# Turning the identity into unread banks at seven places on TensorE, in a graph layer with edge messages, linear attention and slice attention

## What is computed

```python
xn = layernorm(x)
# edges: a filter from the attributes, times the gathered row, summed by source node
filt = silu(attr @ Wf1 + bf1) @ Wf2 + bf2
agg  = segment_sum(xn[dst] * filt, src)
h    = silu(agg @ Wu1 + bu1) @ Wu2 + bu2
x1   = x + xn + batchnorm(h) + linear_attention(xn) * gate(xn) @ Wproj + bproj
# slices: 8 heads, each with 64 slice tokens, over all nodes
x2   = layernorm(x1)
w    = softmax((x2 @ W_x + b_x) @ W_slice / temp)      # nodes x (8 x 64)
tok  = w.T @ (x2 @ W_fx) / sum(w)                      # slice tokens
attn = softmax((tok @ W_q) @ (tok @ W_k).T / 8)
out  = x1 + (w @ (attn @ (tok @ W_v))) @ W_out + b_out
```

## Time and profile before

| | us |
|---|---|
| median of three runs | 2088.68 |
| lowest and highest of them | 2083.26, 2089.93 |
| the profiled execution's own time | 2100.86 |
| its span, from first to last instruction | 2099.1 |
| TensorE busy | 1882.4 (90%) |
| GpSimd busy | 1443.0 (69%) |
| mean granted TensorE clock | 0.956 |

### The profile page before, as it was taken

The page is one execution under the profiler, slowest core; times in us unless marked ns, Lnnn a source line. Parts: engine busy times, 40 slices in busy tenths (PEclk is TensorE's granted clock), DMA queues, the critical chain, the costliest instruction groups (busy, mean ns, idle before and its releaser), DMA issues. The chain is left out here.

```text
span 2099.1 us, 38406 instructions
## 1 busy us (share of the span) xinstructions
PE 1882.4 (90%) x9844; PEld 1548.4 (74%) x9844; DVE 1501.5 (72%) x3453; ACT 1332.9 (63%) x2412; POOL 1443.0 (69%) x997
## 2 busy tenths in 40 slices
PE   5989999999989998998899889999997298799998
PEld 3667888787778787777777777877786276577778
DVE  6967877777777767776777677776775287788846
ACT  4547776776677667666766576667664067577733
POOL 2216888888888888888888888888888564355600
PEclk9999999999999999999999999999999599699979
DMA  9888888988988798878988898888897793000002
GB/s 370 319 299 169 162 159 166 173 159 143 172 165 160 137 172 168 157 140 162 176 146 154 156 177 142 157 159 167 150 158 115 202 322 120 12 0 0 0 31 103
DMA packets 288979, 325.41 MB, mean 155 GB/s; under 512 B 30118, under 2 KB 251721, under 8 KB 288688
## 3 DMA queue, kind: packets, MB, share of 16 engines
q0 software_dynamic: 112896, 102.81, 40.0%
q1 hardware_dynamic: 172576, 217.21, 32.4%
q10 hardware_dynamic: 3280, 2.83, 0.5%
HBM read 167.64 MB, written 154.97 MB: 154 GB/s over the span
## 5 line engine op out<-in xcount | busy, mean ns | idle before, releaser
L994 POOL DMA_INDIRECT sums<-x_rows,out_idx x784 | 1226.3, 1564 | 288.3 <-issue 207.2
L1048 PE MATMUL bank<-wf,x_rows 128*128 128x256 f32 x3136 | 800.5, 384 | 0.0
L1048 PEld LDWEIGHTS bank<-wf,x_rows 128*128 128x128 f32 x3136 | 545.2, 192 | 54.3
L1172 ACT ACTIVATE x_rows<-bank,bf 128x512 f32<-128x512 f32 x392 | 270.4, 690 | 279.8 <-PE bank L1026 277.1
L1268 DVE TENSOR_TENSOR msg_low<-bank,msg_high 128x512 fp32r<-128x512 f32 x392 | 271.3, 692 | 162.0 <-ACT msg_high L1192 162.0
L1299 DVE TENSOR_TENSOR bank<-bank,x_rows 128x512 f32<-128x512 f32 x392 | 272.7, 696 | 119.4 <-PE bank L1048 114.5
L1046 PE MATMUL bank<-gnn_bf_halves,ones 128*128 128x256 f32 x784 | 296.5, 378 | 0.0
L1192 ACT ACTIVATE msg_high<-bank 128x512 fp32r<-128x512 f32 x392 | 234.3, 598 | 88.5 <-DVE bank L1299 85.8
L1180 ACT ACTIVATE x_rows<-pair 128x516 f32<-128x516 f32 x392 | 234.1, 597 | 63.7 <-DMA sums<-x_rows,out_idx 62.9
L1199 ACT ACTIVATE x_rows<-bank 128x512 f32<-128x512 f32 x392 | 235.2, 600 | 36.9 <-PE bank L1036 33.4
L1036 PE MATMUL bank<-window,spread 128*128 128x256 f32 x784 | 193.2, 328 | 58.2 <-DVE spread L1263 37.2
(11 more groups left out here) (331 smaller groups left out, 2740.2 us busy)
## 6 DMA issues: line engine op xcount, KB each, us to landing
window<-xn_halves SPq DMA_DIRECT2D x392, 128.0 KB, 4.2
sums<-gate SPq DMA_DIRECT2D x32, 800.0 KB, 10.8
x_rows<-id_rows SPq DMA_DIRECT2D x98, 256.0 KB, 5.0
x_rows<-attr_rows SPq DMA_DIRECT2D x98, 256.0 KB, 4.7
xn_halves<-xn_halves SPq DMA_DIRECT2D x7, 1792.0 KB, 7.3
x_rows<-id_rows SPq DMA_DIRECT2D x98, 128.0 KB
sums<-x_rows,out_idx POOLq DMA_INDIRECT x784
res<-sums SPq DMA_DIRECT2D x24, 512.0 KB, 7.7
```

The costliest lines, as they stand in the source:

```text
L994: nc.gpsimd.indirect_dma_start(g.sums_dram[k], bass.IndirectOffsetOnAxis(ap=out_idx[:, ET * c + t:ET * c + t + 1], axis=0), summed[c % 2][ ...
L1048: mm = T.matmul(out, hidT[:, j // 2, f, ds((2 * (j % 2) + t) * P, P)], g.wf2[:, f, :], start=False, stop=f == CB - 1)
L1172: A.activation(hidT[:, h, f, :], hps[:], ACT.Silu, bias=g.bf1[:, f:f + 1]).then_inc(hid_ready, 1)
```

## The change

A new helper turns the identity into a bank that nobody reads at that time, so many times in a row. It is called at seven places on TensorE; nothing else is altered. No instruction waits for these turns, and they give no semaphore. The line numbers behind each place shift by up to 13.

```diff
+def keep_warm(nc, g, bank, n):
+    for _ in range(n):
+        nc.tensor.transpose(bank[:, 0:P], g.ident[:], g.ident[:])
@@ opening, tensor
             gram_group(NG - 1)
+            keep_warm(nc, g, turn[0], 12)
@@ messages_and_attention, tensor
+            keep_warm(nc, g, fps[1], 6)
             hidden(0, 0, 0, 0)
@@ update_nodes, tensor, behind the turns of line 1612
                     mm.then_inc(back_made, 1)
+            keep_warm(nc, g, turn[0], 32)
@@ slice_tokens, tensor
             for t in range(NT - LAG, NT):
+                keep_warm(nc, g, tps, 8 if t == NT - LAG else 3)
                 turn_w(t, t % RING)
                 tokens(t, t % RING)
@@ slice_attention_and_output, tensor
                 mm = T.matmul(g.ps[0][0:FD, ds(q * P, P)], mean_of[:], diag[:, ds(q * P, P)], start=True, stop=True)
             mm.then_inc(mat, 1)
+            keep_warm(nc, g, g.ps[5], 8)
             pe.wait_ge(vec, FX_DONE)
...
                 mm = T.transpose(g.ps[5][0:FG, ds(k * P, P)], at[:, ds(k * FG, FG)], g.ident[:])
             mm.then_inc(mat, 1)
+            keep_warm(nc, g, g.ps[4], 6)
             pe.wait_ge(vec, BACK)
...
                 if h % 4 == 3:
                     mm.then_inc(mat, 1)
+            keep_warm(nc, g, g.ps[4], 6)
             for u in range(NT):
```

## The result

The changed kernel takes 2082.82 us (median of 22 runs, 2079.16 to 2095.09). The kernel before, run in turn with it on the same chip, takes 2091.68 us (22 runs, 2081.98 to 2099.41). The ratio is 0.9966, 95% interval 0.9951 to 0.998, so 4.2 to 10.2 us less, 7.1 by the ratio. The forecast was -9.5 us. The two fastest runs differ by 2.8 us, the medians by 8.9: what goes is above all the slow part of the spread.

A forecast was written before the change was run, and what follows sets the result against it. GpSimd bounds the edge loop; TensorE's stream, slowed by low clock, bounds the attention's last third. Attention -8.5, opening -1, update and tail 0 sum to -9.5 us, carried to the median 2088.68: 2079.2 us, stated range 2073 to 2089.

The forecast's parts named there:

- the attention term: Slice attention: eight turns in the `fxT` wait keep the clock from falling at 2006, so later products run faster; -8.5 us.
- the cover: Ahead of the output products: six turns (0.65) and four products (0.47) fit inside the 1.49 us wait, costing nothing.
- Opening, -1: Twelve turns behind the opening, six ahead of the edge loop: first scatter sooner, -1 us, bounds -3.5 and +2.6.
- Later and shorter: Edge loop's start: the clock still falls behind the six turns, but later and for less than the 10.1 us before.
- 32 turns, 0: Behind the update: clock is low again when the tokens begin, so 0 us; bounds -5.6 and +1.
- the tokens' tail, 0: Eight and three turns in the tokens' tail: clock is 1.00 there anyway, so 0 us, at most +0.3.
- The clock holds and falls soon after: Rival, attention: 64-row products too weak to hold the clock after 2006; about 2086.5 us, chance 0.2.
- My price of nothing: Attention's two groups of six turns lie in covered waits and cost nothing; at the low clock 0.5 and 0.6 us.
- Less to win in most runs: Rival, attention: the median run may have no low stretch, leaving only the opening's -1; about 2087.7 us, chance 0.12.
- Turns do not count: Rival, all seven places: the 81 turns do not raise or hold the clock; about +0.7, 2089.4 us, chance 0.06.
- The 32 turns hold up the block's end: Rival, update's end: turns at the low clock delay it, +1.0 us; with nothing won elsewhere 2089.7 us, chance 0.12.

The follow-up runs named there:

- third group: Beside the kernel before (2087.31 us): four products in the `fxT` wait, 2087.99 us; products at all seven places, 2082.55; changed kernel with four products for the eight turns, 2084.81.
- Eight turns alone: Kernel before plus only the eight identity turns in the slice attention's wait for `fxT`: 2087.30 us, ratio 0.9975.
- four products alone: Kernel before plus only four full identity products in the `fxT` wait: one execution 2089.51 us; timed again 2087.99 us, ratio 1.0.
- six and six alone: Kernel before plus only the attention's two groups of six turns, behind line 2331 and ahead of the output products, `fxT` wait unfilled: 2090.26 us, ratio 0.9998.
- the probe: Kernel before plus 32 identity turns, then 24 products of 64 rows, while TensorE waits for the edge loop's last scatters: one execution, 2094.23 us.

## Why the prediction was right

The direction, the place and the mechanism of the attention term were right; the gain was 7.1 us by the ratio, where 9.5 was forecast. That the median of 2082.82 lies so near to 2091.68 - 9.5 = 2082.2 is partly luck, since the ratio gives less than the 8.9 between the medians.

**Attention, -8.5.** Measured in the pair of profiles: 88.67 - 96.80 = -8.13. By its steps: lines 2319 and 2326 together -3.6 (said -3.9), line 2331 with the copy behind it -0.4 (-0.4), line 2338 to the first output product -1.1, and from there to the second group -0.6 (together -1.7; said -1.8 and 0), line 2356 -2.4 (-2.4). The split of the third pair is as the cover said it would be: the six turns put the first output product 0.65 us later, which takes that much from the -1.8, and the wait behind it gives it back, 0.86 us for 1.49. The parts were sized from the earlier trace rows alone, by 0.117 to 0.21 us a product at the two levels, and that ratio held.

Two readings of the prediction were loose, and neither enters its sum: 25 turns in 5.80 busy us are 0.23 us each and not 0.22, and the edge loop is 0.71 of the span (1480 of 2099 us) and not three quarters.

**Opening, -1.** -0.6 in the profile from the first product to the first scatter (14.38 to 13.79). Over all profiled executions: seven without turns there have 14.16 us on average (13.71 to 14.53), the five with the 12 and 6 have 13.23 (12.24 to 13.90), so -0.9, in ranges that overlap. "Later and shorter" is what the windows show.

**32 turns, 0, and the tokens' tail, 0.** Both right in this pair of profiles. The stretch from the first token turn to the steady tokens is 19.1 us in both, and the block's end keeps its 0.35 us. Over all profiles, from the first token turn to the attention's first product it takes 188.6 to 191.9 us, with and without turns there, so the zero is known to some 3 us. The comparison of the third group (5.4 us from products at all seven places over the one wait) says that the places outside the attention may be worth more than the 1 that the sum gives them.

**The rivals.** *The clock holds and falls soon after*: false for the changed kernel. Eight turns alone fell for 3.3 us at the start of the output products, at a price of 1.3 us; the two executions with four products alone did not fall, and the one that is comparable took as long from the `fxT` wait to the end as with the six and six, 80.1 us. So the six and six are at most a guard against a fall that comes in some executions. My price of nothing for them holds where it does not come. *Less to win in most runs*: true in part. The mechanism is real (six and six alone kept the clock through an unfilled wait), in one of four profiles. The forecast carried the attention term from one slow execution, in which the clock had fallen, to the median, as if it fell in every run; that is the likeliest part of its excess. An estimate from the profiles, three quarters of 8.1 and the opening's 0.9, is 7.0 beside the 7.1 of the ratio, but that this fits is luck as far as these runs go: four profiles say little of how often it falls, and where only the attention is filled three quarters of 8.1 would be 6.1 us, while the ratios stand for 4.0, 5.2 and 0.0. *Turns do not count*: false; the probe's turns brought the clock from 0.50 to 1.00 in 5.1 us, and turns and products give the same ratio, 0.9966. *The 32 turns hold up the block's end*: false, they ran at 1.00.

What is not shown is how the 7.1 us divide. Fillings in the attention alone have ratios of 0.9981, 0.9975 and 1.0, all seven places 0.9966, 0.9966 and 0.9984, and all but the attention 1.0003 (0.9975 to 1.0031, so up to 5 us faster is not excluded). The third group shows that products at all places beat the one wait, by 5.4 us (3.2 in the other kernel of that kind, within the spread); which of them does it is open, since in the profiles only the opening's 0.9 can be seen. Nor is it shown what in an execution places a wait so that the clock falls.

## What to carry to other kernels

Where a serial stage of TensorE falls to the low clock behind a short wait, fill that wait first: look for 0.50 in the windows, read what TensorE did just before it, and ask whether the stretch behind it is a pure stream of TensorE. Don't take the places that look worthless in one profile for worthless: here the kernel with products at all places was 5.4 us faster than the one with only the best place filled. Filling that runs in a wait costs nothing here, whether turns or products of 128 rows, but there is an end to it: 39 us less at the low clock bought no more that could be measured than 28 us did. A gain of this kind takes away the slow part of the spread, so take many runs and look at the highest and the lowest, not at one median or one profile.

## What the hardware showed that I had not expected

- Products with 64 rows did not bring the clock up in 10.5 dense us, where 32 turns of 128 rows needed under 5.1. But the clock stayed up over them where it was up: 3.6 us of line 2337 ran at 1.00 behind the filled wait.
- The same instructions around the same 1.49 us wait leave the clock at 1.00 in one execution and at 0.50 for 17 to 20 us in three others.
- One execution ran its 588 output products 0.113 us apart, where all others, of the same program too, have 0.118. The windows of TensorE over 66 us of it (the single execution of four products):

```profile
2013.00:2079.00 66.00, 65.50 (x575) 1.00 0.23 81
```

The same window of the same program again:

```profile
2013.00:2079.00 66.00, 65.88 (x559) 1.00 0.23 81
```

16 products more in the same time, at the same granted 1.00. It belongs to the execution, since the program is the same; its cause stays open. An attention of 86.06 us there is 88.66 less these 2.6, and not a gain of the products.
